# A third bank for a block's product, the product moved ahead of the short matmuls in passes 3 and 4, and one check moved into pass 3

## The reference, cut to what matters

```python
msg = x[src]
agg = jax.ops.segment_sum(msg, dst, num_segments=n_nodes)        # SAGE, twice
...
m = jnp.concatenate([x[dst_f], x[src_f], ea_f], axis=1) @ W.T + b
agg = jax.ops.segment_sum(m, dst_f, num_segments=n)              # three times
return jax.nn.relu(agg)
...
h = jax.nn.relu(_batchnorm(h, g0, be0))
```

## Time and profile before

| | |
|---|---|
| median of 3 runs | 1188.8 us (1186.09 to 1193.02) |
| profiled execution, its own time | 1187.27 us |
| its span, first to last instruction | 1185.5 us |
| mean granted clock of TensorE | 0.925 |
| TensorE busy | 1057.4 us, 89% |
| VectorE busy | 732.1 us, 62% |
| ScalarE busy | 344.2 us, 29% |
| DMA queue of SP | 39.4% of 16 engines' span |

### The profile page before, as it was taken

One profiled execution on the slowest core, in us unless ns is written; L12 is line 12 of the kernel. 1 busy time (PEld: TensorE's weight loads), 2 busy tenths in 40 slices (PEclk: granted clock), 3 DMA queues, 4 the chain that ended last, 5 costly groups with the idle time before them and its releaser, 6 DMA issues. The chain is left out here.

```text
span 1185.5 us, 21103 instructions
## 1 busy us (share of the span) xinstructions
PE 1057.4 (89%) x8433; PEld 658.1 (56%) x8433; DVE 732.1 (62%) x1499; ACT 344.2 (29%) x649; POOL 104.2 (9%) x125
## 2 busy tenths in 40 slices
PE   0248999999999997999999999996899998899993
PEld 0248988989999984545555444443344444344442
DVE  5798999999999853633434755444554554333444
ACT  1555556655666530200000011113310105100000
POOL 4121111222211110000000000000000000000001
PEclk9758988988898897999999999997899998899997
DMA  6334545646455348973775436745036755036750
GB/s 160 55 109 148 172 131 202 206 144 215 128 171 168 106 163 266 410 263 127 295 292 208 175 118 255 291 161 217 14 120 234 285 189 218 19 122 260 289 189 21
DMA packets 67163, 216.85 MB, mean 183 GB/s; under 512 B 32032, under 2 KB 45083, under 8 KB 53523
## 3 DMA queue, kind: packets, MB, share of 16 engines
q1 hardware_dynamic: 59044, 164.49, 39.4%
q0 software_dynamic: 8016, 50.95, 11.7%
HBM read 170.67 MB, written 44.74 MB: 182 GB/s over the span
## 5 line engine op out<-in xcount | busy, mean ns | idle before, releaser
L1293 PE MATMUL PM<-Aring,Xop 128*128 128x512 fp8e4 (+1 forms) x1960 | 398.5, 363 | 0.0
L1293 PEld LDWEIGHTS PM<-Aring,Xop 128*128 128x128 f16 x1960 | 181.5, 98 | 216.6 <-issue 16.3
L1293 PE MATMUL PM<-Ares,Xop 128*128 128x512 fp8e4 x588 | 137.6, 389 | 2.2 <-ACT Xop L1855 1.4
L1816 ACT ACTIVATE F<-PH,bag 64x512 f32<-64x512 f32 (+1 forms) x39 | 25.5, 658 | 382.4 <-PE PH L1512 382.4
L772 PE MATMUL PW<-Aring 128*128 128x52 fp8e4 (+3 forms) x2151 | 115.3, 217 | 20.3 <-ACT F L836 16.7
L772 PEld LDWEIGHTS PW<-Aring 128*128 128x128 fp8e4 x2151 | 111.5, 103 | 23.3 <-ACT F L836 18.0
L785 PE MATMUL PA<-Ares,ea 128*128 128x32 f16 x1867 | 112.3, 235 | 0.0
L1649 DVE TENSOR_SCALAR S<-PM 128x256 f32<-128x256 f32 (+1 forms) x75 | 31.4, 418 | 130.7 <-PE PM L1293 119.2
L785 PEld LDWEIGHTS PA<-Ares,ea 128*128 128x128 f16 x1867 | 108.4, 116 | 0.0
L1293 PEld LDWEIGHTS PM<-Ares,Xop 128*128 128x128 f16 x588 | 56.0, 100 | 73.1 <-issue 10.8
L836 ACT ACTIVATE F<-PW 128x392 uint16<-128x392 f32 x196 | 85.0, 506 | 6.2 <-PE PW L772 3.9
(11 more groups left out here) (149 smaller groups left out, 1113.4 us busy)
## 6 DMA issues: line engine op xcount, KB each, us to landing
Aring<-adj SPq DMA_DIRECT2D x72, 1568.0 KB, 9.8
adj<-Aring POOLq DMA_DIRECT2D x12, 1568.0 KB, 6.0
adj<-Xop POOLq DMA_DIRECT2D x12, 1568.0 KB, 6.2
Ares<-adj SPq DMA_DIRECT2D x6, 1568.0 KB, 22.3
rc<-ea_sum SPq DMA_DIRECT2D x36, 128.0 KB, 5.6
eaf<-in_erow SPq DMA_DIRECT2D x62, 51.0 KB
Aring<-adj SPq DMA_DIRECT2D x4, 784.0 KB, 4.5
rc<-rc_d SPq DMA_DIRECT2D x12, 256.0 KB, 10.3
```

The lines of the kernel that those rows point to most:

```text
L1293: last = nc.tensor.matmul(o, x[:, h, :], rhs, start=h == 0, stop=h == NT - 1)
L1816: nc.scalar.activation(F[0:64, c:c + w], PH[b % 2][0:64, 0:w], ACT.Relu, bias=t["bag"][:, 4 + conv:5 + conv]).then_inc(s_hr, 1)
```

## The change

It has four parts. A product goes to `PM[b % 3]`, three banks; the bank `PC`, which served two tiny matmuls in pass 4, is gone, and these go to `PB`. `main(b)` waits for `sums(b-3)`. In passes 3 and 4 `main(i+1)` stands at step i for i below 7, so `main(2)` comes before `post(0)`, `main(3)` before `post(1)`, and so on to `main(7)` before `post(5)`; step 7 has no product (`post(6)` follows `post(5)`), and from step 8 on the order is the old one. The check of block 12 moves from the end of pass 2 to step 1 of pass 3 on VectorE, and the load of block 4 for pass 3, which must wait for it, from the end of pass 2 to the start of pass 3.

```diff
+CAUGHT = 7
...
-            "PM": [ps(f"PM{i}", [128, 512]) for i in range(2)],
-            "PC": ps("PC", [128, 512]),
+            "PM": [ps(f"PM{i}", [128, 512]) for i in range(3)],
...
+        if p == 3 and not slow:
+            sp.wait_ge(t["s_ck"], CHECKED.index((2, NB - 1)) + 1)
+            for h in range(2):
+                sp.dma_start(t["Aring"][:, ring(RB + 1)[0], h, :], m["adj"][2 * (RB + 1) + h]).then_inc(
+                    t["s_ar"][ring(RB + 1)[0]][h], 16)
         for b in range(NB):
...
                 sp.wait_ge(t["s_mm"], mm0 + b + 1)
+                if (p, b) == (2, NB - 1):
+                    continue
...
             a = landed(pe, b)
-            if b >= 2:
-                pe.wait_ge(s_S, b - 1)
+            if b >= 3:
+                pe.wait_ge(s_S, b - 2)
             multiply(nc, t, a, Xop, b, range(NT))
...
         for i in range(NB + 2):
-            if p >= 1 and (1 if p < 3 else 2) <= i < NB and not slow:
+            if p in (1, 2) and 1 <= i < NB and not slow:
                 main(i)
+            if p >= 3 and not slow and 1 <= i < NB and i != CAUGHT:
+                main(i + 1 if i < CAUGHT else i)
             if 1 <= i <= NB:
                 post(i - 1)
...
             if i >= lag + 1:
                 rest(i - lag - 1)
+            if p == 3 and i == 1:
+                check(NB - 1, 2)
             if i < NB and (p, i) != (2, NB - 1):
-                check(i)
+                check(i, p)
...
-        if p == 2:
-            check(NB - 1)
```

More of the change, by code:

```diff
@@ L1095, in general @@
     rows = 17 if p < 0 else 64
-    flat = [x[0:rows, :] for x in t["PM"]] + [t["PC"][0:rows, :]] + [x[0:rows, :] for x in t["PH"]]
+    flat = [x[0:rows, :] for x in t["PM"]] + [x[0:rows, :] for x in t["PH"]]
     flat += [x[0:rows].rearrange("p a b -> p (a b)") for x in t["PG"]]
@@ L1288, in multiply @@
             rhs = a.rearrange("p s (h d) -> p s h d", h=NT)[:, :, h, :]
-            o = t["PM"][b % 2][:, 0:n].rearrange("p (s d) -> p s d", s=2)
+            o = t["PM"][b % 3][:, 0:n].rearrange("p (s d) -> p s d", s=2)
         else:
             rhs = a[:, 0, 0:NT * n].rearrange("p (h d) -> p h d", h=NT)[:, h, :]
-            o = t["PM"][b % 2][:, 0:n]
+            o = t["PM"][b % 3][:, 0:n]
         last = nc.tensor.matmul(o, x[:, h, :], rhs, start=h == 0, stop=h == NT - 1)
@@ L1301, in propagate @@
     S, rc, hT, dd, sq, stt = (t[k] for k in ("S", "rc", "hT", "dd", "sq", "st"))
-    PM, PC, PH, PG = t["PM"], t["PC"], t["PH"], t["PG"]
+    PM, PB, PH, PG = t["PM"], t["PB"], t["PH"], t["PG"]
     conv, slow = p - 2, type(block) is Stage
@@ L1330, in tiles, with ring @@
         return (4, 128) if b < NB - 1 else (1, 128)
-    def ring(b):
+    def ring(b, p=p):
         i = (NB - RB) * (p - 1) + b - RB
@@ L1454, in _, with landed @@
             g.wait_ge(s_o[1], 16 * 6)
-    def landed(engine, b):
+    def landed(engine, b, p=p):
         if b < RB:
@@ L1460, in landed @@
             return t["Ares"][:, b]
-        i, k = ring(b)
+        i, k = ring(b, p)
         engine.wait_ge(t["s_ar"][i][0], 16 * k)
@@ L1479, in tell @@
                 pe.wait_ge(s_tot, 1)
-                nc.tensor.matmul(PC[0:1, 0:4], m["scl"][:, 3:4], t["dsum"][:, 7, :], start=True, stop=True)
-                nc.tensor.matmul(PC[0:1, 4:12], m["scl"][0:16, 3:4], t["csum"][:].rearrange("p a i -> p (a i)"), start=True,
+                nc.tensor.matmul(PB[0:1, 0:4], m["scl"][:, 3:4], t["dsum"][:, 7, :], start=True, stop=True)
+                nc.tensor.matmul(PB[0:1, 4:12], m["scl"][0:16, 3:4], t["csum"][:].rearrange("p a i -> p (a i)"), start=True,
                                  stop=True).then_inc(s_told, 1)
@@ L1557, in remaining @@
                 for h in range(NT):
-                    last = nc.tensor.matmul(PM[b % 2][:, st % 2 * SW:st % 2 * SW + n], Xop[:, h, :], of[:, h, :],
+                    last = nc.tensor.matmul(PM[b % 3][:, st % 2 * SW:st % 2 * SW + n], Xop[:, h, :], of[:, h, :],
                                             start=h == 0, stop=h == NT - 1)
@@ L1643, in sums @@
                     stored = fused and RANK[(c + h) // SW] < EARLIER
-                    of = by_quad(sraw[:, c + h:c + h + w] if stored else PM[b % 2][:, h:h + w])
+                    of = by_quad(sraw[:, c + h:c + h + w] if stored else PM[b % 3][:, h:h + w])
                     if p <= 1:
@@ L1658, in sums, with check @@
                                                ALU.add, ALU.mult).then_inc(s_r, 1)
-        def check(b):
+        def check(b, p):
             if slow or (p, b) not in CHECKED:
                 return
-            a = landed(v, b)
+            a = landed(v, b, p)
             r = next(i for i, (q, blocks) in enumerate(ROUNDS) if q == p and b in blocks)
@@ L1690, in tell @@
                 v.wait_ge(s_told, 1)
-                own(nc.vector.tensor_copy(fl[:, 0:12], PC[0:1, 0:12]))
+                own(nc.vector.tensor_copy(fl[:, 0:12], PB[0:1, 0:12]))
                 own(nc.vector.tensor_tensor(fl[:, 4:8], fl[:, 4:8], fl[:, 8:12], ALU.add))
```

## The result

| | before | after |
|---|---|---|
| median | 1187.44 us (1184.02 to 1193.02, 4 runs) | 1205.84 us (1203.03 to 1207.72, 4 runs) |
| span of the profiled execution | 1185.5 us | 1203.4 us |
| end of pass 2's short matmuls | 807.02 us | 808.06 us |
| from there to the end of the folded products | 39.3 us | 34.9 us |
| pass 3, from there to its last short matmul | 140.5 us | 160.3 us |

The ratio of after to before is 1.016 [1.0131, 1.0189]: slower, by 1.6%. The forecast was 1197.0 us with a range of 1190 to 1202, so the direction is right and the size is not. The stages are read from TensorE's timeline, as in the prediction; they say more than the totals, because the program up to the end of pass 2 does the same in every kernel here and still ends anywhere from 802.2 to 813.7 us. Pass 3 took nearly what was forecast (161 us). The seam gained its 4.4 us.

A forecast was written before the change was run, and what follows sets the result against it. TensorE was taken to bound the passes, so only their seams could be won. Terms -14.4 - 4.8 + 28.0 = +8.8 us on 1187.3 us gave 1196.1, moved half way towards the 1.5 us higher median to 1197.0 us; range 1190 to 1202.

The forecast's parts named there:

- Part 1: Start of passes 3 and 4: TensorE's wait for VectorE's factors and the slow clock behind it go, gaining 14.4 us.
- Part 2: Seam behind pass 2: engines no longer wait for the check of block 12, gaining 4.8 us.
- rival D: Seam behind pass 2: something else ends it, so moving block 12's check gains nothing; 1201 us, chance 0.04.
- Both fit: Early pass 3: block 4's load lands before main(4) is due, and block 1's check and sums finish before post(1).
- Part 3: Third product bank, and PB in place of PC: no wait for a bank to remove, so no gain.
- Part 4: Pass 3: late checks delay loads, stalling blocks 5, 7 and 9; 21.4 us plus 6.6 us slow clock, 28.0 us lost.
- Rival A: Pass 3: loads land in 10.2 us, stalls are shorter, the third may spare the clock; 1191.8 us, chance 0.15.
- the 10.2 to 12.0 us: Ring loads: time for a pair of DMAs to land, read from profile rows; the forecast took 10.9 us.
- Rival B: Pass 3: checks end within 3.5 us of the product, no load is late, only gains stay; 1168.1 us, chance 0.07.
- Rival C: Pass 3: late loads share engines with the next, landing up to 5 us later three times; 1211 us, chance 0.03.

The follow-up runs named there:

- g1_caught2: Changed kernel with only main(2) ahead of post(0), then the old product order, plus reordered VectorE checks and later block 4 load in pass 3; 1169.68 us, ratio 0.986 to before.
- r4_check_first: Changed kernel with VectorE in pass 3 taking the check of block i ahead of the statistics of block i-2; 1185.44 us, ratio 0.998 to before.
- r1_root_first: Changed kernel with ScalarE in pass 4 taking the square root of block b-2 ahead of the ReLU of block b; 1193.83 us, ratio 1.0052 to before.
- h2_before_root: Kernel before the change, with only the root of block b-2 put ahead of the ReLU of block b on ScalarE in pass 4; 1184.13 us, ratio 0.9988.
- h1_depth7: Changed kernel, product order kept, with VectorE's checks and block 4's load reordered in pass 3 and ScalarE's root first in pass 4; 1165.76 us, ratio 0.9837 to before.
- r3_no_checks: Changed kernel without the additions of pass 3's checks (blocks 1, 3, 5, 7, 9, 11); 1177.16 us, ratio 0.9912 to before.
- r2_pass3_old: Changed kernel with TensorE's old order of products in pass 3 alone; 1191.49 us, ratio 1.0021 to before.

## Why the prediction was right or wrong

- **Part 1, the start of passes 3 and 4, 7.4 + 7.0 us.** Right in kind and size. Free of later losses, pass 3 takes 132.7 us for 140.5 (7.8) and pass 4 takes 140.1 for 147.3 (7.2, g1_caught2). In the changed kernel the second gain did not reach the end.
- **Part 2, 4.8 us at the seam.** 4.4 us measured, 34.9 us for 39.3; rival D is out. "Both fit, so the move costs nothing, with 1 us to spare" was too short a look: `post(1)` waited just 0.31 us, but the sums of blocks 1 and 2 that piled up kept VectorE busy until 869.57 and so held the check of block 3 too.
- **Part 3.** No wait for a bank came or went, as said.
- **Part 4, pass 3.** Stalls of 7.5, 6.7 and 5.8 us for 7.9, 7.5 and 6.0, together 20.0 for 21.4. The slow clock behind them: the products of blocks 5, 7 and 9 took 2.7, 2.5 and 2.0 us over 10.75, 7.1 us for 6.6. The sum is 27.1 for 28.0. The mechanism holds for blocks 7 and 9 (r4_check_first). For block 5 it is one of two bounds: VectorE's backlog, which the prediction left out of this sum, ended 0.05 us after the ReLU. That it ended no later, and so left the size right, is luck; and moving the statistics alone did not remove this stall (6.62 us in r4_check_first). Had I also worked out the check's start from what VectorE has to do, I would have found it.
- **The step that failed** is the last sentence of Part 4: "Pass 4 has no checks, so its loads start with the products' ends and it loses nothing". It lost 1.6 us before the product of block 6 and 3.4 us before the short matmuls of block 6, and 3.3 us more by the clock: that product took 12.42 us for 10.75, and these short matmuls with the transposes behind them 3.84 us for 2.26. That is 8.3 us, which used up the gain of 7.2. What the runs showed in place of "loses nothing": ScalarE's order, the root behind the ReLU, holds the sums back, and with them a load (r1_root_first takes 11.1 us off the pass, of which h2_before_root shows 2.6 to be older than the change). With the 8.3 us the forecast would have been 1205.3 us, against 1205.84 measured. Behind the end of pass 2, +8.8 + 8.3 = +17.1 us compares with 395.3 - 378.5 = 16.8 in the traces; the terms' own errors, up to 1 us each, cancel in part. I had followed the one chain from the short matmuls to the checks, and not looked for others that start there. A sign was at hand: the prediction's "Within a pass TensorE stands still nowhere" is not so, since at the end of pass 4 before it waits 0.59 and 2.03 us, for the sums behind this same root.
- **Rival A** asked for stalls 0.7 us shorter and no slow clock at the third. They were 0.4, 0.8 and 0.2 us shorter, and the clock fell each time. The products started 10.5, 10.2 and 10.6 us after the issue of their pairs (issues at 878.32, 913.19 and 947.94, starts at 888.84, 923.35 and 958.50), at the lower end of the 10.2 to 12.0 us. Those two bounds come from the first two rows, not from the first and the last; the last, 12.5 us, is of a pair issued 4.7 us behind another. The Trainium skill, DMA: Bandwidth & Descriptors, section "Anatomy of one DMA — SWDGE (gpsimd) path", led to an estimate of 9.4 us; the traces are 0.8 to 1.2 us above it, so the measurement decides. That section is about DMAs that GpSimd issues, and these go out from SyncE.
- **Rival B** (a check that starts before the moved matmuls matter gives 1168.1 us) was rightly held unlikely for the diff as it is. Made true by hand, in h1_depth7, it gives 1165.76 us, with the root's own 2.6 us within.
- **Rival C** would have had stalls of over 10 us; none was.

## What to carry to other kernels

When instructions of one engine are put later, list everything on every other engine that stands, in program order, behind an instruction that waits for them, and follow each chain until it reaches a load or comes back to the first engine. Here there were two such chains, matmuls to ReLU to statistics to check to load, and matmuls to ReLU to root to layer norm to sums to factors to load. A long wait that costs next to nothing before (here up to 10.9 us at a reciprocal, 72.6 us in all, of which 2.6 us reached TensorE) can mark such a chain: the order of instructions fits only the order it was written for. Here the cure in pass 4 was to exchange two instructions.

## What the runs showed of the hardware

A short wait can cost clock too. TensorE stood still 1.61 us before the product of block 6 in pass 4, and the granted clock (the first of the last three columns) was full until then and fell behind it:

```profile
1088.00:1090.00 2.00, 1.73 (x8) 0.49 (x6) 0.00 (x0) 0.62 (x2) 0.00 (x0) 1.00 1.06 452
1090.00:1092.00 2.00, 0.66 (x4) 0.33 (x5) 1.71 (x6) 0.16 (x2) 0.77 (x1) 1.00 0.11 44
1092.00:1096.00 4.00, 4.00 (x12) 1.50 (x11) 3.33 (x8) 0.00 (x0) 0.00 (x0) 0.57 0.43 106
1096.00:1100.00 4.00, 4.00 (x20) 1.83 (x19) 0.00 (x0) 0.00 (x0) 0.00 (x0) 1.00 0.97 408
```

0.50 is 1.2 GHz, so for most of 1092 to 1096 TensorE ran at the lower of its two levels, and the product took 1.67 us longer: the price was as high as the wait. In r3_no_checks and r4_check_first waits of 1.67 and 1.80 us at the same place were followed by the same 12.42 us. But in r2_pass3_old a wait of 1.81 us there cost nothing, at a granted clock of 1.00 throughout:

```profile
1081.72 10.73 PE L1293 MATMUL PM<-Aring,Xop 128*128 128x512 fp8e4 x49 [1.81 <-issue]
```

Pass 4 of that kernel took 148.6 us all the same. The wait of 3.42 us later in the pass cost it 2.6 us of clock, where the one of 3.43 us in the changed kernel cost 1.6; its waits and slow clock add up to 8.2 us, in other parts than the 8.3 us above.

Nor does the price rise steadily with the wait: 5.80, 6.70 and 7.49 us in pass 3 cost 2.0, 2.5 and 2.7 us, but 6.52 us before the product of block 9 in r1_root_first cost 1.5 (12.22 us for 10.75). Waits of 0.3 to 0.5 us before a product left it at 10.73 or 10.74 us in every trace. So the length of a wait alone does not tell what it costs in clock; what else decides it is open here.
